# Three cross attentions: how the exponents of the rescaling factors reach all 512 columns

## The chip, the cores and the metric

The kernel runs on one core of one Trainium2 chip. The metric is the time of one execution on the device in microseconds (us); the kernel before was timed three times, and the figure is the median. Lower is better.

## The reference, cut to what matters

The network has four layers, each with a cross attention, a self attention and a feed-forward part; 128 rows of width 256 are updated in place. Three of the four cross attentions (layers 0, 1 and 3) are softmax attentions of the 128 rows over a context of 12544 rows, with 16 heads of width 16. Layer 1 has a key mask; layer 3 turns two columns of the queries before the scores. The reference of layer 1:

```python
qm = _split_heads(q @ Wq.T + bq)
km = _split_heads(k @ Wk.T + bk)
vm = _split_heads(v @ Wv.T + bv)
scores = jnp.einsum('bnlh,bnph->bnlp', qm, km) / np.sqrt(HEAD_DIM).astype(np.float32)
scores = jnp.where(attention_mask[:, None, None, :], scores, MASK_FILL)
attn = jax.nn.softmax(scores, axis=-1)
out = jnp.einsum('bnlp,bnph->bnlh', attn, vm)
```

## The kernel before, in words

One class, `CrossAttention`, computes the three softmax cross attentions, one after the other. The context is cut into 49 chunks of 256 rows. A chunk is projected to keys and values on TensorE (L829, L833). For the softmax a running maximum per query and head is kept: rough scores, made from the rounded queries and keys by 32-row matmuls, four at once in the four row strips of the array (`pe_batch`, L861), are reduced by VectorE (L1288). The exact scores follow six steps later (`pe_unit`, L910, eight units of 512 columns per chunk), ScalarE takes their exponential out of PSUM (L1050), and 17-column matmuls add the weighted values and the sums of the weights to an accumulator that stays in one PSUM bank (`pe_attend`, L946).

The maximum that the scores are shifted by is renewed once in a block of four chunks. One block costs these steps, and the change is in them:

- VectorE, `update_shift`: the maximum over the block (L1297), the shift in two exact halves (L1301, L1302), their sum (L1303), the difference from the last shift (L1307), and that difference in two rounded halves (L1308, L1309). All these are 128x16. The last one sets the semaphore `stage_ready`.
- TensorE, `pe_turned` (L921): the 64 columns of `stage` (two rounded halves of the difference, two exact halves of the shift) are transposed into a PSUM bank.
- ScalarE, `act_turned` (L1085): one copy takes the result to `stage_T` and sets `e_drained`.
- SyncE, `load_shift`: a DMA copies rows 32 to 63 of `stage_T` (the shift) into the packed queries of the next block.
- TensorE, `pe_factor` (L930): four matmuls with 32 rows of `stage_T` as the stationary operand and a 0/1 matrix `spread` as the moving one copy the difference of each head to 32 columns.
- ScalarE, `act_factor` (L1093): its exponential, the factor; VectorE, `rescale` (L1318): the accumulator times the factor.

The order on each engine is written out by hand in `tensor`, `scalar`, `vector` and `gpsimd`. The units (eight of scores, and in every fourth step one "turned" and one "factor") go to two PSUM banks in the order of a list, E_BANK, and a unit waits until the unit before it in its bank is drained by ScalarE (`pe_bank_free`). In a step with a turn, one of the two banks holds in this order score unit 1, turned, score unit 4, factor, score unit 7; the other one score units 0, 2, 3, 5, 6. ScalarE drains in the order turned, units 3, 4, 5, values (L1075), factor, unit 6, unit 7. GpSimd splits each chunk's context (L1204, L1207) and keys (L1222, L1224) into a rounded half and a rest. With 13 blocks there are 13 turns and 12 factors in each cross attention; the last two of each come after the context has been projected. Steps with a turn and a factor while the context is still projected: 10 in each of the three, 30 in all; they are called turn steps below.

In layer 1 (the masked one) VectorE also makes the keys (L1330) and their fill rows; TensorE adds fill terms (L856).

## Time and profile before

| | us |
|---|---|
| median of 3 runs | 1737.86 (1735.96 to 1740.72) |
| the profiled execution, its own time | 1728.72 |
| span of the profiled execution | 1726.9 |
| busy in the span: PE 1569.3 (91%), DVE 1021.3 (59%), ACT 954.8 (55%), POOL 697.5 (40%) | |

PE is TensorE's matmuls, PEld its weight loads, DVE VectorE, ACT ScalarE, POOL GpSimd. A matmul is in flight for longer than it keeps the array from the next one, so the time of a row of matmuls is read from the starts, not from the sum of the durations. In rows a shape such as 32*128 32x256 means 32 rows by 128 columns stationary, 256 columns moving. The three cross attentions concerned lie at about 10 to 440 us, 550 to 985 us and 1255 to 1665 us of the span.

### The profile page before, as it was taken

What the parts mean: (1) busy time and instruction counts of PE and PEld (TensorE: products, weight loads), DVE (VectorE), ACT (ScalarE), POOL (GpSimd) and SP (SyncE); (2) the same over time, 40 slices, a digit from 0 to 9 for tenths busy, and PEclk for the clock granted to TensorE, in tenths of its full rate; (3) what the DMA queues carried; (4) which work ended last, traced back from release to release, by engine and by line L of the source; (5) the groups of instructions that cost most, each with busy time, mean ns of one, the idle gap of its engine ahead of it and who ended that gap; (6) DMA issues with size and microseconds to landing.
All of it is one profiled execution on the core that took longest, in us unless ns stands there. A gap on an engine that the chain in (4) does not pass through costs nothing. (4 is left out here: it accounts for less than half of the span.)

```text
span 1726.9 us, 48550 instructions
## 1 busy us (share of the span) xinstructions
PE 1569.3 (91%) x19973; PEld 1362.8 (79%) x19973; DVE 1021.3 (59%) x1427; ACT 954.8 (55%) x1834; POOL 697.5 (40%) x625
## 2 busy tenths in 40 slices
PE   6999999999777999999999897987499999999965
PEld 5888888888556888888888686876388888888852
DVE  7667787774446877667766252013576666666622
ACT  4677777777313466666666522211167777777742
POOL 5655555551004655555553000000275555555202
PEclk9999999999977999999999998978699999999986
DMA  7665555554045676555554345590365555555430
GB/s 179 176 185 131 127 133 125 127 125 102 1 157 121 182 202 152 143 139 138 142 141 117 96 168 189 202 326 15 95 171 148 135 133 128 131 130 133 102 104 4
DMA packets 149245, 235.42 MB, mean 136 GB/s; under 512 B 24200, under 2 KB 64516, under 8 KB 148100
## 3 DMA queue, kind: packets, MB, share of 16 engines
q1 hardware_dynamic: 141090, 225.09, 49.8%
q10 hardware_dynamic: 7938, 7.23, 1.6%
q8 instruction: 161, 2.64, 0.6%
q14 instruction: 56, 0.46, 0.1%
HBM read 107.06 MB, written 0.23 MB: 62 GB/s over the span
## 5 line engine op out<-in xcount | busy, mean ns | idle before, releaser
L1288 DVE TENSOR_REDUCE L_xattn_maxima<-L_xattn_ps 128x4 f32<-128x1024 f32 x588 | 691.2, 1218 | 337.9 <-PE L_xattn_ps L861 334.1
L1050 ACT ACTIVATE L_xattn_p_ring<-L_xattn_ps 128x512 f32<-128x512 f32 x1176 | 677.6, 598 | 301.5 <-PE L_xattn_ps L910 286.1
L910 PE MATMUL L_xattn_ps<-L_xattn_q_packed,L_xattn_k_packed 128*128 128x256 f32 x2352 | 457.8, 298 | 8.6 <-ACT L_xattn_p_ring L1050 4.7
L910 PEld LDWEIGHTS L_xattn_ps<-L_xattn_q_packed,L_xattn_k_packed 128*128 128x128 f32 x2352 | 337.9, 190 | 65.0 <-issue 29.6
L946 PE MATMUL L_xattn_ps<-L_xattn_p_ring,L_xattn_v_ring 128*17 128x128 f32 x9408 | 289.3, 273 | 1.0 <-ACT L_xattn_p_ring L1050 1.0
L1222 POOL TENSOR_TENSOR L_xattn_k_ring<-L_xattn_k_full,consts 128x512 fp32r<-128x512 f32 x147 | 154.7, 1053 | 279.2 <-ACT L_xattn_k_full L1063 157.8
L829 PE MATMUL L_xattn_ps<-L_xattn_ctx_halves,L_xattn_w_halves 128*128 128x256 f32 x1764 | 261.5, 286 | 0.5 <-POOL L_xattn_ctx_halves L1207 0.4
L946 PEld LDWEIGHTS L_xattn_ps<-L_xattn_p_ring,L_xattn_v_ring 128*17 128x17 f32 x9408 | 242.4, 97 | 23.6 <-ACT L_xattn_p_ring L1050 1.6
L833 PE MATMUL L_xattn_ps<-L_xattn_w_halves,L_xattn_ctx_halves 128*128 128x256 f32 x1764 | 259.9, 285 | 0.0
L829 PEld LDWEIGHTS L_xattn_ps<-L_xattn_ctx_halves,L_xattn_w_halves 128*128 128x128 f32 x1764 | 233.7, 194 | 3.7 <-issue 1.8
L833 PEld LDWEIGHTS L_xattn_ps<-L_xattn_w_halves,L_xattn_ctx_halves 128*128 128x128 f32 x1764 | 232.6, 192 | 2.2 <-issue 0.4
L1204 POOL TENSOR_TENSOR L_xattn_ctx_halves<-L_xattn_ctx_chunk,consts 128x512 fp32r<-128x512 f32 x129 | 134.4, 1042 | 212.6 <-PE L_xattn_ps L833 123.5
L1207 POOL TENSOR_TENSOR L_xattn_ctx_halves<-L_xattn_ctx_chunk,L_xattn_ctx_halves 128x512 fp32r<-128x512 f32 x147 | 190.1, 1293 | 17.9 <-ACT L_xattn_ctx_halves L1128 7.7
L1224 POOL TENSOR_TENSOR L_xattn_k_ring<-L_xattn_k_full,L_xattn_k_ring 128x512 fp32r<-128x512 f32 x147 | 191.0, 1300 | 11.5
L861 PE MATMUL L_xattn_ps<-L_xattn_k_ring,L_xattn_q_hi 32*128 32x256 f32 x2352 | 148.9, 312 | 11.5 <-DVE L_xattn_maxima L1288 7.8
L861 PEld LDWEIGHTS L_xattn_ps<-L_xattn_k_ring,L_xattn_q_hi 32*128 32x128 f32 x2352 | 108.7, 186 | 44.5 <-issue 15.6
L1075 ACT ACTIVATE L_xattn_v_ring<-L_xattn_ps 128x512 f32<-128x512 f32 x147 | 88.0, 599 | 57.2 <-PE L_xattn_ps L833 37.0
L1063 ACT ACTIVATE L_xattn_k_full<-L_xattn_ps,weights 128x256 f32<-128x256 f32 x196 | 81.7, 472 | 12.8 <-PE L_xattn_ps L829 12.8
L233 POOL TENSOR_SCALAR L_attn_rstd<-L_attn_mean_var 128x1 f32<-128x1 f32 x4 | 0.9, 223 | 190.6 <-DVE L_attn_mean_var L222 190.6
L856 PE MATMUL L_xattn_ps<-L_xattn_fill_rows,L_xattn_fill_terms 2*128 2x512 f32 x392 | 52.2, 501 | 3.9 <-DVE L_xattn_maxima L1288 2.1
L1318 DVE TENSOR_TENSOR L_xattn_ps<-L_xattn_ps,L_xattn_factor 128x512 f32<-128x512 f32 x36 | 24.9, 691 | 50.7 <-PE L_xattn_ps L946 50.7
L1330 DVE SCALAR_TENSOR_TENSOR L_xattn_k_full<-L_xattn_ps,weights,L_xattn_mask_chunk 128x256 f32<-128x256 f32 x98 | 42.6, 475 | 1.4 <-PE L_xattn_ps L829 1.0
(365 smaller groups left out, 1109.2 us busy)
## 6 DMA issues: line engine op xcount, KB each, us to landing
L_xattn_k_packed<-L_xattn_k_ring SPq DMA_DIRECT2D x588, 128.0 KB, 2.4
L_xattn_ctx_chunk<-in_ctx_chunks SPq DMA_DIRECT2D x147, 256.0 KB, 3.2
L_xattn_k_packed<-L_xattn_k_ring SPq DMA_DIRECT2D x588, 64.0 KB, 2.1
L_ffn_W<-in_experts_W SPq DMA_DIRECT2D x16, 1024.0 KB, 12.8
L_xattn_mask_chunk<-L_xattn_mask ACTq DMA_DIRECT2D x49, 128.0 KB, 3.1
L_xattn_ctxT<-in_ctxT SPq DMA_DIRECT2D x7, 896.0 KB, 8.5
L_xattn_ctx<-in_ctx SPq DMA_DIRECT2D x7, 896.0 KB, 7.0
weights<-in_pack_L_attn SPq DMA_DIRECT2D x10, 512.0 KB, 4.3
```

What stands on the lines that cost most here:

```text
L829: last = pe.matmul(L.ps[:, KV_BANK, d * KEYS:(d + 1) * KEYS], wk[:, b, e, d * P:(d + 1) * P], x[:, a, e, :], start=start, stop=stop, skip_ ...
L833: last = pe.matmul(L.ps[:, self.v_bank(n), t * D:(t + 1) * D], x[:, a, e, t * P:(t + 1) * P], wv[:, b, e, :], start=start, stop=stop, skip ...
L861: last = pe.matmul(bank[:, r, k * KEYS:(k + 1) * KEYS], self.q_hi[own, 8 * d + 2 * r + k, :], self.k_ring[own, slot, 0, d, :], start=not s ...
L910: last = pe.matmul(L.ps[:, bank, d * 2 * S:(d + 1) * 2 * S], self.k_packed[s][:, quarter, d, half * P:(half + 1) * P], q[:, 2 * pair:2 * p ...
L946: last = pe.matmul(L.ps[q:q + DH + 1, ACC_BANK, col:col + S], self.v_ring[:, m % V_RING, half, h, :], self.p[t % P_RING][:, at, :], start= ...
L1050: act.activation(self.p[t % P_RING][:, 4 * quarter:4 * quarter + 4, :], L.ps[:, E_BANK[unit], :].rearrange("p (h n) -> p h n", n=S), ACT.Exp)\
L1075: act.activation(self.v_ring[:, n % V_RING, :, :, 0:DH].rearrange("p t h n -> p (t h) n"), L.ps[:, self.v_bank(n), :].rearrange("p (m n) - ...
L1204: pool.tensor_tensor(hi, self.ctx_chunk[c][:, :, :], wide(ones[:, 0:DC], KEYS), ALU.mult)\
L1207: pool.tensor_tensor(lo, self.ctx_chunk[c][:, :, :], hi.bitcast(F32), ALU.subtract)\
L1222: pool.tensor_tensor(hi, k[:, :, :], wide(ones[:, 0:DC], KEYS), ALU.mult).then_inc(L["k_hi_ready"], 1)
L1224: pool.tensor_tensor(lo, k[:, :, :], hi.bitcast(F32), ALU.subtract).then_inc(L["k_lo_ready"], 1)
L1288: dve.tensor_reduce(out[:, 4 * v:4 * v + 4], L.ps[:, M_BANK + 2 * v:M_BANK + 2 * v + 2, :] .rearrange("p b (k n) -> p (b k) n", k=2), AX_X ...
```

## The change

The difference of the shifts is now split exactly into three bfloat16 parts on VectorE (five small operations instead of three). It is no longer part of the transposed `stage`, which shrinks to 32 columns with the shift alone. The three parts lie in a 128x128 bfloat16 tile `delta_parts` (five of its eight groups of 16 columns are zero); in all blocks but the first a bfloat16 matmul against the identity transposes it into the same PSUM bank, behind the transpose of `stage`. ScalarE takes the bank out with two copies: `stage_T` (which now sets a semaphore of its own, `stage_turned`, for the DMA) and `delta_T`, 128x128 in bfloat16, which sets `e_drained`. The four matmuls of `pe_factor` read all 128 rows of `delta_T` and a bfloat16 `spread` of 128 rows, whose making at the start of layer 0 takes one more operation on VectorE.

```diff
--- before.py
+++ after.py
@@ -155,7 +155,7 @@
         self.causal_bf = ctx.enter_context(nc.sbuf_tensor("causal_bf", [P, 4, P], BF16))
         self.causal_T_bf = ctx.enter_context(nc.sbuf_tensor("causal_T_bf", [P, 4, P], BF16))
         self.zeros_bf = ctx.enter_context(nc.sbuf_tensor("zeros_bf", [P, BANK], BF16))
-        self.spread = ctx.enter_context(nc.sbuf_tensor("spread", [2 * H, H, 32], F32R))
+        self.spread = ctx.enter_context(nc.sbuf_tensor("spread", [P, H, 32], BF16))
         self.x = ctx.enter_context(nc.sbuf_tensor("x_rows", [S, D], F32))
         self.kv = ctx.enter_context(nc.sbuf_tensor("feature_sums", [64, D + 1], F32))
         self.turn = ctx.enter_context(nc.sbuf_tensor("turn", [P, 24], F32))
@@ -609,10 +609,13 @@
         self.p_ring = sb("p_ring", [P, P_RING, H, S])
         self.p = [self.p_ring[:, c, :, :] for c in range(P_RING)]
         self.maxima = sb("maxima", [S, BLOCK + 2, H])
-        self.shift = sb("shift", [S, 3, H])
-        self.stage = sb("stage", [S, 64])
+        self.shift = sb("shift", [S, 2, H])
+        self.stage = sb("stage", [S, 2 * H])
+        self.delta = sb("delta", [S, 2, H])
+        self.delta_parts = sb("delta_parts", [S, 8, H], BF16)
+        self.delta_T = sb("delta_T", [P, S], BF16)
         self.warm = sb("warm", [P, 2])
-        self.stage_T = sb("stage_T", [64, S], F32R)
+        self.stage_T = sb("stage_T", [2 * H, S], F32R)
         self.factor = sb("factor", [P, 4 * S])
 
         self.q_pairs = self.p_ring[:, 0:2, :, :]
@@ -688,8 +691,11 @@
     def load_shift(self, sp, b):
 
         L = self.L
-        sp.wait_ge(L["e_drained"], E_AT["turned", b] + 1)
-        sp.dma_start(self.q_packed[b % 2][96:98, :, :].bitcast(F32), self.stage_T[32:64, :].bitcast(F32))\
+        if b:
+            sp.wait_ge(L["stage_turned"], b)
+        else:
+            sp.wait_ge(L["e_drained"], E_AT["turned", b] + 1)
+        sp.dma_start(self.q_packed[b % 2][96:98, :, :].bitcast(F32), self.stage_T[:, :].bitcast(F32))\
           .then_inc(L["shift_loaded"], 16)
 
     def fill_tails(self, sp):
@@ -918,8 +924,11 @@
         L, unit = self.L, E_AT["turned", b]
         pe.wait_ge(L["stage_ready"], b + 1)
         self.pe_bank_free(pe, unit)
-        pe.transpose(L.ps[0:64, E_BANK[unit], 0:S], self.stage[:, :], self.net.const("identity"))\
-          .then_inc(L["e_filled"], 1)
+        last = pe.transpose(L.ps[0:2 * H, E_BANK[unit], 0:S], self.stage[:, :], self.net.const("identity"))
+        if b:
+            last = pe.matmul(L.ps[:, E_BANK[unit], S:2 * S], self.delta_parts[:, :, :].rearrange("p a h -> p (a h)"),
+                             self.net.ident_bf[:, :], start=True, stop=True, skip_group_check=True)
+        last.then_inc(L["e_filled"], 1)
 
     def pe_factor(self, pe, b):
 
@@ -929,7 +938,7 @@
         for i in range(4):
             last = pe.matmul(L.ps[:, E_BANK[unit], i * S:(i + 1) * S],
                              self.net.spread[:, 4 * i:4 * i + 4, :].rearrange("p h n -> p (h n)"),
-                             self.stage_T[0:2 * H, :], start=True, stop=True, skip_group_check=True)
+                             self.delta_T[:, :], start=True, stop=True, skip_group_check=True)
         last.then_inc(L["e_filled"], 1)
 
     def pe_attend(self, pe, m, half):
@@ -1082,7 +1091,11 @@
         act.wait_ge(L["e_filled"], unit + 1)
         if b:
             act.wait_ge(L["shift_loaded"], 16 * b)
-        act.activation(self.stage_T[:, :], L.ps[0:64, E_BANK[unit], 0:S], ACT.Copy).then_inc(L["e_drained"], 1)
+        last = act.activation(self.stage_T[:, :], L.ps[0:2 * H, E_BANK[unit], 0:S], ACT.Copy)
+        if b:
+            last.then_inc(L["stage_turned"], 1)
+            last = act.activation(self.delta_T[:, :], L.ps[:, E_BANK[unit], S:2 * S], ACT.Copy)
+        last.then_inc(L["e_drained"], 1)
 
     def act_factor(self, act, b):
 
@@ -1103,7 +1116,10 @@
         if self.first:
             identity = net.const("identity")
             dve.tensor_copy(net.ident_bf[:, :], identity).then_inc(L["constants_made"], 1)
-            dve.tensor_tensor(net.spread[:, :, :], wide(identity[0:2 * H, 0:H], 32), wide(identity[0:2 * H, H:2 * H], 32),
+            dve.tensor_tensor(self.delta_T[:, 0:H], identity[:, 0:H], identity[:, H:2 * H], ALU.add)\
+               .then_inc(L["parts_placed"], 1)
+            dve.wait_ge(L["parts_placed"], 1)
+            dve.tensor_tensor(net.spread[:, :, :], wide(self.delta_T[:, 0:H], 32), wide(identity[:, 2 * H:3 * H], 32),
                               ALU.add).then_inc(L["constants_made"], 1)
             dve.tensor_copy(net.causal_bf[:, :, :], times(net.const("causal"), 4)).then_inc(L["constants_made"], 1)
             dve.tensor_copy(net.causal_T_bf[:, :, :], times(net.const("causal_T"), 4)).then_inc(L["constants_made"], 1)
@@ -1292,21 +1308,23 @@
 
         L, stage, first = self.L, self.stage, b % 2
         most = self.maxima[:, (BLOCK + 1) * (1 - first), :]
-        one, two = stage[:, 32:48].bitcast(F32R), stage[:, 48:64].bitcast(F32R)
+        one, two = stage[:, 0:H].bitcast(F32R), stage[:, H:2 * H].bitcast(F32R)
         dve.wait_ge(L["batch_reduced"], 4 * min(BLOCK * (b + 1), NCHUNK))
         o.after(dve.tensor_reduce(most, self.maxima[:, first:first + BLOCK + 1, :].rearrange("p s h -> p h s"), AX_X,
                                   ALU.max))
         if b:
             dve.wait_ge(L["e_filled"], E_AT["turned", b - 1] + 1)
         o.after(dve.tensor_scalar(one, most, -1.0, None, ALU.mult))
-        o.after(dve.scalar_tensor_tensor(two, most, -1.0, stage[:, 32:48], ALU.mult, ALU.subtract))
-        last = dve.tensor_tensor(self.shift[:, b % 2, :], stage[:, 32:48], stage[:, 48:64], ALU.add)
+        o.after(dve.scalar_tensor_tensor(two, most, -1.0, stage[:, 0:H], ALU.mult, ALU.subtract))
+        last = dve.tensor_tensor(self.shift[:, b % 2, :], stage[:, 0:H], stage[:, H:2 * H], ALU.add)
         if b:
             o.after(last)
-            delta = self.shift[:, 2, :]
+            delta, rest, parts = self.delta[:, 0, :], self.delta[:, 1, :], self.delta_parts
             o.after(dve.tensor_tensor(delta, self.shift[:, b % 2, :], self.shift[:, 1 - b % 2, :], ALU.subtract))
-            o.after(dve.tensor_copy(stage[:, 0:H].bitcast(F32R), delta))
-            last = dve.tensor_tensor(stage[:, H:2 * H], delta, stage[:, 0:H], ALU.subtract)
+            o.after(dve.tensor_copy(parts[:, 0, :], delta))
+            o.after(dve.tensor_tensor(rest, delta, parts[:, 0, :], ALU.subtract))
+            o.after(dve.tensor_copy(parts[:, 1, :], rest))
+            last = dve.tensor_tensor(parts[:, 2, :], rest, parts[:, 1, :], ALU.subtract)
         last.then_inc(L["stage_ready"], 1)
         dve.wait_ge(L["stage_ready"], b + 1)
 
@@ -1354,7 +1372,7 @@
         if not self.dequantizing:
             self.norm.vector_rows(dve)
         self.net.wait_weights(dve, L.name)
-        dve.memset(self.stage[:, 0:32], 0.0)
+        dve.memset(self.delta_parts[:, :, :], 0.0)
         o.after(dve.memset(self.maxima[:, :, :], -LARGEST))
         dve.wait_ge(L["q_in_psum"], 1)
         if self.turned:
```

TensorE around one turn and factor, layer 0, step of the second turn, before (`stage` is transposed by L921, the factor's exponents are made by L930):

```order
L946 MATMUL L_xattn_ps<-L_xattn_p_ring,L_xattn_v_ring 17x128 x32
L921 MATMUL L_xattn_ps<-consts,L_xattn_stage 64x128
L910 MATMUL L_xattn_ps<-L_xattn_q_packed,L_xattn_k_packed 128x256 x4
L833 MATMUL L_xattn_ps<-L_xattn_w_halves,L_xattn_ctx_halves 128x256 x6
L910 MATMUL L_xattn_ps<-L_xattn_q_packed,L_xattn_k_packed 128x256 x2
L833 MATMUL L_xattn_ps<-L_xattn_w_halves,L_xattn_ctx_halves 128x256 x6
L930 MATMUL L_xattn_ps<-L_xattn_stage_T,spread 128x128 x4
L910 MATMUL L_xattn_ps<-L_xattn_q_packed,L_xattn_k_packed 128x256 x2
```

and the same place now:

```order
L955 MATMUL L_xattn_ps<-L_xattn_p_ring,L_xattn_v_ring 17x128 x32
L927 MATMUL L_xattn_ps<-consts,L_xattn_stage 32x128
L929 MATMUL L_xattn_ps<-ident_bf,L_xattn_delta_parts 128x128
L916 MATMUL L_xattn_ps<-L_xattn_q_packed,L_xattn_k_packed 128x256 x4
L839 MATMUL L_xattn_ps<-L_xattn_w_halves,L_xattn_ctx_halves 128x256 x6
L916 MATMUL L_xattn_ps<-L_xattn_q_packed,L_xattn_k_packed 128x256 x2
L839 MATMUL L_xattn_ps<-L_xattn_w_halves,L_xattn_ctx_halves 128x256 x6
L939 MATMUL L_xattn_ps<-L_xattn_delta_T,spread 128x128 x4
L916 MATMUL L_xattn_ps<-L_xattn_q_packed,L_xattn_k_packed 128x256 x2
```

One matmul has come in behind the transpose; nothing else has changed its place.

VectorE in the step before, where the shift is renewed, before:

```order
L1297 TENSOR_REDUCE L_xattn_maxima<-L_xattn_maxima 128x16
L1301 TENSOR_SCALAR L_xattn_stage<-L_xattn_maxima 128x16
L1302 SCALAR_TENSOR_TENSOR L_xattn_stage<-L_xattn_maxima,L_xattn_stage 128x16
L1303 TENSOR_TENSOR L_xattn_shift<-L_xattn_stage 128x16
L1307 TENSOR_TENSOR L_xattn_shift<-L_xattn_shift 128x16
L1308 CAST L_xattn_stage<-L_xattn_shift 128x16
L1309 TENSOR_TENSOR L_xattn_stage<-L_xattn_shift,L_xattn_stage 128x16
```

and now:

```order
L1313 TENSOR_REDUCE L_xattn_maxima<-L_xattn_maxima 128x16
L1317 TENSOR_SCALAR L_xattn_stage<-L_xattn_maxima 128x16
L1318 SCALAR_TENSOR_TENSOR L_xattn_stage<-L_xattn_maxima,L_xattn_stage 128x16
L1319 TENSOR_TENSOR L_xattn_shift<-L_xattn_stage 128x16
L1323 TENSOR_TENSOR L_xattn_delta<-L_xattn_shift 128x16
L1324 CAST L_xattn_delta_parts<-L_xattn_delta 128x16
L1325 TENSOR_TENSOR L_xattn_delta<-L_xattn_delta,L_xattn_delta_parts 128x16
L1326 CAST L_xattn_delta_parts<-L_xattn_delta 128x16
L1327 TENSOR_TENSOR L_xattn_delta_parts<-L_xattn_delta,L_xattn_delta_parts 128x16
```

The chain that ends with `stage_ready` is two operations longer, and each waits for the one before it.

ScalarE in the turn step, before:

```order
L1085 ACTIVATE L_xattn_stage_T<-L_xattn_ps 64x128
L1050 ACTIVATE L_xattn_p_ring<-L_xattn_ps 128x512 x3
L1075 ACTIVATE L_xattn_v_ring<-L_xattn_ps 128x32x16
L1093 ACTIVATE L_xattn_factor<-L_xattn_ps 128x512
L1050 ACTIVATE L_xattn_p_ring<-L_xattn_ps 128x512 x4
```

and now:

```order
L1094 ACTIVATE L_xattn_stage_T<-L_xattn_ps 32x128
L1097 ACTIVATE L_xattn_delta_T<-L_xattn_ps 128x128
L1059 ACTIVATE L_xattn_p_ring<-L_xattn_ps 128x512 x3
L1084 ACTIVATE L_xattn_v_ring<-L_xattn_ps 128x32x16
L1106 ACTIVATE L_xattn_factor<-L_xattn_ps 128x512
```

The second copy stands in front of the exponential of unit 3.

## Rows read from the trace of the kernel before

**Rows 1.** Busy time over 60:405, 605:950 and 1300:1630, the sum of the three.
```profile
sum 1020.00, PE 1015.04 PEld 907.39 DVE 710.13 ACT 704.17 POOL 545.95; mean PE 338.35 PEld 302.46 DVE 236.71 ACT 234.72 POOL 181.98
```

**Rows 2.** By line L1085 and L1309: durations (min/median/max), and waiters (us, times).
```profile
  PEld L_xattn_ps L910: 9.5, 30
...
L1309 DVE TENSOR_TENSOR L_xattn_stage<-L_xattn_shift,L_xattn_stage x36: 174/176/1062, 74.6 to 1640.6; 128x16 f32<-128x16 f32 x36
...
  PEld L_xattn_ps L921: 2.3, 10
```

**Rows 3.** TensorE in order of time, turn step of layer 0 (start, us, group).
```profile
108.56 0.30 PE L921 MATMUL L_xattn_ps<-consts,L_xattn_stage 128*64 128x128 f32 x1
...
109.56 0.87 PE L833 MATMUL L_xattn_ps<-L_xattn_w_halves,L_xattn_ctx_halves 128*128 128x256 f32 x6
...
111.32 0.66 PE L930 MATMUL L_xattn_ps<-L_xattn_stage_T,spread 32*128 32x128 f32 x4
...
112.78 0.51 PE L910 MATMUL L_xattn_ps<-L_xattn_q_packed,L_xattn_k_packed 128*128 128x256 f32 x2
113.12 0.64 PE L829 MATMUL L_xattn_ps<-L_xattn_ctx_halves,L_xattn_w_halves 128*128 128x256 f32 x4
```

**Rows 4.** TensorE, the step after it, without a turn.
```profile
117.69 0.74 PE L910 MATMUL L_xattn_ps<-L_xattn_q_packed,L_xattn_k_packed 128*128 128x256 f32 x4
118.28 0.88 PE L833 MATMUL L_xattn_ps<-L_xattn_w_halves,L_xattn_ctx_halves 128*128 128x256 f32 x6
...
121.06 0.64 PE L829 MATMUL L_xattn_ps<-L_xattn_ctx_halves,L_xattn_w_halves 128*128 128x256 f32 x4
```

**Rows 5.** ScalarE in the turn step of rows 3.
```profile
108.89 0.27 ACT L1085 ACTIVATE L_xattn_stage_T<-L_xattn_ps 64x128 fp32r<-64x128 f32 x1 [0.98 <-PE L_xattn_ps L921]
109.13 1.29 ACT L1050 ACTIVATE L_xattn_p_ring<-L_xattn_ps 128x512 f32<-128x512 f32 x2
...
112.01 0.60 ACT L1093 ACTIVATE L_xattn_factor<-L_xattn_ps 128x512 f32<-128x512 f32 x1
```

**Rows 6.** ScalarE and TensorE in a turn step of layer 1.
```profile
711.69 0.60 ACT L1093 ACTIVATE L_xattn_factor<-L_xattn_ps 128x512 f32<-128x512 f32 x1
...
712.69 0.50 PE L910 MATMUL L_xattn_ps<-L_xattn_q_packed,L_xattn_k_packed 128*128 128x256 f32 x2
```

**Rows 7.** VectorE and GpSimd before the turn of rows 3.
```profile
107.50 0.18 DVE L1309 TENSOR_TENSOR L_xattn_stage<-L_xattn_shift,L_xattn_stage 128x16 f32<-128x16 f32 x1
...
107.51 1.08 POOL L1222 TENSOR_TENSOR L_xattn_k_ring<-L_xattn_k_full,consts 128x512 fp32r<-128x512 f32 x1 [1.87 <-ACT L_xattn_k_full L1063]
```

**Rows 8.** VectorE and GpSimd before the turn at 241.5, layer 0.
```profile
240.45 0.99 DVE L1309 TENSOR_TENSOR L_xattn_stage<-L_xattn_shift,L_xattn_stage 128x16 f32<-128x16 f32 x1
...
240.38 1.04 POOL L1222 TENSOR_TENSOR L_xattn_k_ring<-L_xattn_k_full,consts 128x512 fp32r<-128x512 f32 x1 [1.90 <-DMA L_xattn_k_packed<-L_xattn_k_ring]
241.49 1.28 POOL L1224 TENSOR_TENSOR L_xattn_k_ring<-L_xattn_k_full,L_xattn_k_ring 128x512 fp32r<-128x512 f32 x1
```

**Rows 9.** VectorE and GpSimd before the turn at 208.3, layer 0.
```profile
207.05 0.90 DVE L1308 CAST L_xattn_stage<-L_xattn_shift 128x16 fp32r<-128x16 f32 x1
207.98 0.17 DVE L1309 TENSOR_TENSOR L_xattn_stage<-L_xattn_shift,L_xattn_stage 128x16 f32<-128x16 f32 x1
208.19 2.35 DVE L1288 TENSOR_REDUCE L_xattn_maxima<-L_xattn_ps 128x4 f32<-128x1024 f32 x2
...
206.84 1.08 POOL L1222 TENSOR_TENSOR L_xattn_k_ring<-L_xattn_k_full,consts 128x512 fp32r<-128x512 f32 x1 [1.62 <-ACT L_xattn_k_full L1063]
208.00 1.30 POOL L1224 TENSOR_TENSOR L_xattn_k_ring<-L_xattn_k_full,L_xattn_k_ring 128x512 fp32r<-128x512 f32 x1
```

**Rows 10.** GpSimd in layer 1, in the turn step of rows 6.
```profile
708.10 1.04 POOL L1222 TENSOR_TENSOR L_xattn_k_ring<-L_xattn_k_full,consts 128x512 fp32r<-128x512 f32 x1 [3.31 <-DVE L_xattn_k_full L1330]
```

**Rows 11.** By line L869: the bfloat16 matmuls with 128 columns near the end of layer 0's cross attention.
```profile
L869 PE MATMUL L_xattn_ps<-causal_bf,ident_bf x16: 219/219/230, 406.1 to 412.0; 128*128 128x128 bf16 x16
```

**Rows 12.** TensorE near the start of layer 0.
```profile
22.18 0.79 PE L861 MATMUL L_xattn_ps<-L_xattn_k_ring,L_xattn_q_hi 32*128 32x256 f32 x4 [2.88 <-DVE L_xattn_maxima L1288]
```

## The prediction

> **What bounds the kernel.** I read the busy times of the three stages first, then TensorE in order of time through one step with a turn and one without, then ScalarE and VectorE beside GpSimd in the same stretch, and the waits of the lines that change.
>
> Over 1020 us of the three softmax cross attentions a matmul is in flight for 1015.0, VectorE is busy for 710, ScalarE for 704, GpSimd for 546 [rows 1]. So in these stages TensorE sets the pace, and what counts is only what makes it start later. The reader should look at starts. In the turn step of layer 0 the stretch from the transpose (108.56) to the next projection (113.12) takes 4.56 us; the same stretch without a turn takes 3.37, from 117.69 to 121.06 [rows 3, 4]. A turn and its factor cost TensorE 1.19 us. Of this 0.41 is the turn: 1.00 us from 108.56 to 109.56 against 0.59 from 117.69 to 118.28 [rows 3, 4]. The factor costs the other 0.78.
>
> TensorE waits in one place of each turn: score unit 4 takes the PSUM bank that the turned block held, and cannot start before ScalarE has copied it out. 30 weight loads waited 9.5 us for that copy, 0.32 each [rows 2]. In 10 turns TensorE waited for VectorE's last operation before the turn as well (2.3 us in all) [rows 2]. Their durations show why: the median is 176 ns, the longest 1062, for 128x16 values. Where it is long, GpSimd was running.
>
> **The factor's matmuls (a gain).** The four 32-row matmuls go from 111.32 on; from the projection before them to the rough scores after them there are a change from 128 rows to 32 and one back. By the starts the whole costs 0.78. In bfloat16 with 128 rows both changes go. What is left are four matmuls of 128 columns; at 128 columns against 256 they need at most what the others do. Bounds for the saving on TensorE: 0.78 at most, nothing at least; I take 0.50 (an estimate: 0.28 stays for four short matmuls, at 0.06 to 0.07 each, half the 0.12 of a 256-column matmul: a group of six takes 0.88, one of four 0.64 [rows 4]).
>
> But this saving runs into ScalarE. Score unit 7 takes the factor's PSUM bank, so it cannot start before the exponential of the factor ends. That starts at 112.01, right behind the drain of the values on ScalarE, which is tied to the projection before the factor and does not come earlier; it ends at 112.61 [rows 5]. With 0.05 for the release (an estimate) unit 7 can start at 112.66. It starts at 112.78 now [rows 3]. Of the 0.50 only 0.12 arrives: 20 turn steps in layers 0 and 3, -2.4 us. In layer 1 the fill matmuls lie between: the exponential ends at 712.29, unit 7 starts at 712.69 [rows 6], and 0.35 arrives: 10 x 0.35 = -3.5 us.
>
> **The second copy (a loss in all 30 turns).** `e_drained` now comes with the second of two copies. One copy takes 0.27, and the next operation on ScalarE starts 0.24 behind it (108.89, 109.13) [rows 5]. TensorE already waits for this copy, with nothing to cover it, so all 0.24 counts. The added matmul delays the first copy: at least by nothing (its own time in flight is 219 ns for such a bfloat16 matmul [rows 11], against 0.30 for the transpose [rows 3]), at most by 0.15, for a change from the narrow transpose to 128 columns. I take 0.06: together +0.30, bounds 0.24 and 0.39. 30 x 0.30 = 9.0 us. The exponentials of units 3 and 4 come later by the same, which TensorE's own delay covers. The DMA of the shift hangs on the first copy and is not later against TensorE.
>
> Here the Trainium skill has a rule that would make it dearer (TensorEngine Tiling (Array Packing), Key Properties): a change of tiling mode drains TensorE. The transpose narrows from 64 columns to 32, the width class of the 17-column matmuls before it, so by the rule one drain would only move behind the transpose; in the trace a turn costs 0.41, of which 0.32 is the wait for the copy, so the narrow transpose and all changes around it cost only 0.09 [rows 2 to 4]. By the rule the upper bound of 0.39 would hold, 2.7 us more in all; no run here shows this pair yet.
>
> **The longer chain on VectorE (a loss in up to 20 turns).** Two more operations of 128x16, at a pitch of 0.21 (207.98 to 208.19) [rows 9]: 0.42. Where nothing disturbs them, this is hidden: before the turn at 108.56 the chain ended at 107.68 [rows 7], 0.88 early [rows 3]. In layer 1 the keys are made behind the chain, and GpSimd starts only after them [rows 10]; there the cover holds and the cost is nothing. In layers 0 and 3 GpSimd starts its split of the keys just as the chain ends. The two do not share: at 240.45 the last operation took 0.99 instead of 0.18, and it ended at 241.44, 0.02 behind GpSimd's 1.04 from 240.38 [rows 8]; a cast started at 207.05 behind GpSimd's start at 206.84 took 0.90 [rows 9]. The next VectorE operation then went in front of GpSimd's second one (207.98 against 208.00), and after that GpSimd runs for 1.28 to 1.30 [rows 8, 9].
>
> So there are two cases, by who is first.
> - *VectorE first* (rows 7: 107.50 against 107.51; 10 turns, those of layers 0 and 3 that did not wait). Now the third of the five operations stands there. The fourth, a cast, waits for the end of GpSimd's 1.08 at 108.59 and ends at 108.62; the fifth slips in before the second GpSimd operation, as at 207.98, and ends at 108.83. With 0.06 to TensorE the turn starts at 108.89 instead of 108.56: +0.33, with the second copy +0.63. The 0.33 is 3.3 us over 10 turns.
> - *GpSimd first* (the 10 turns that waited). The third operation ends at 241.44, the fourth goes in front of GpSimd's second one (241.49), the fifth is held until that ends: 241.49 + 1.28 + 0.03 = 242.80, where the chain ended at 241.44 before. +1.36 on a wait that already has no cover: 10 x 1.36 = 13.6 us.
>
> The Trainium skill has this as a rule (SBUF — State Buffer, SBUF: two separate sides): VectorE operations with two SBUF inputs or in a two-port mode and GpSimd operations exclude each other for whole instructions, whoever comes first. It also counts a cast among the operations that take the pair; the rows show this for a cast to fp32r only. Were a cast to bfloat16 free, the first case would cost 0.21 less each, 2.1 us in all; the second one would not change, since its fifth operation has two inputs.
>
> **The rest.** At the start of layer 0 one more VectorE operation stands before the first reductions, for which TensorE waited 2.88 us at 22.18 [rows 12]. At least 0.1; at most one more held operation, 1.3 as above. I take 0.8. The six turns and factors behind the last projection: TensorE gains 0.2 to 0.5 on a factor, and waits for the longer copy; nothing, between -1 and +1. The width of `stage` and the zeroing cost nothing that shows.
>
> **Sum.** 9.0 + 3.3 + 13.6 - 2.4 - 3.5 + 0.8 = +20.8 us. The profiled execution took 1728.7, so it would take 1749.5; the median of the runs is 9.1 above that execution, and the same difference on 1737.9 gives 1758.7. I predict 1759.
>
> **Rivals.**
> - *VectorE first in all 20 turns of layers 0 and 3.* The order is decided by 0.01 us (107.50 and 107.51), so it can tip. 9.0 + 20 x 0.33 - 5.9 + 0.8 = +10.5: 1748. Against: before the change 10 of 20 lost, in the same phase. 15 in 100.
> - *GpSimd first in nearly all 20.* 9.0 + 20 x 1.36 - 5.1 = +31: 1769. Same argument the other way. 12 in 100.
> - *The added operations are not held* (a small bfloat16 cast or difference passes beside GpSimd). Then the chain is longer by 0.42 only, hidden in the first case: 9.0 + 10 x 0.42 - 5.9 + 0.8 = +8: 1746. Against: the row of the cast. 8 in 100.
> - *No change:* the chain is covered everywhere and the second copy costs 0.24: 7.2 - 5.9 = +1.3, 1739. It needs a VectorE that starts the chain earlier; in 10 turns it is already late. 8 in 100.
> - *Faster:* unit 7 does not wait for the factor's exponential, because the drain of the values comes earlier than I think, and the whole 0.50 arrives in 30 steps: -15.0, with 9.0 for the copies -6: 1732. It decides as soon as unit 7 starts less than 0.05 behind the factor's exponential. Against: the exponential starts where the drain ends, not where the last factor matmul ends. It also needs the chain on VectorE to be hidden. 6 in 100.
>
> The forecast itself has 51 in 100; its own range, with the bounds of the copies (-1.8, +2.7), the cast (-2.1), the start (-0.7, +0.5), the tails (1) and two turns tipping either way (2), is 1754 to 1764. The range for 8 in 10 takes in the first two rivals: 1745 to 1771. A measurement of this kernel can tell 0.3% (5.2 us) from no change. Faster by more: 0.07. Within: 0.11. Slower: 0.82.
>
> **What would show it.** Right: the wait of unit 4's weight load for the second copy near 0.6 us in each of the 30 turns; `delta_T` starting 0.24 behind `stage_T`; the last operation of the chain (L1327) with a longest duration near 1.1 to 1.3 us and ten or so TensorE waits for it of about 1.4 us; unit 7 right behind the factor's exponential. Blocks of four steps in layer 1 as long as before. Wrong: the four factor matmuls followed by a unit 7 that does not wait; no long duration in the chain although GpSimd runs; a turn pitch in layers 0 and 3 that is the one of before.

## The result, and the profile after

| | before | changed |
|---|---|---|
| median of 20 runs, us | 1737.84 (1732.89 to 1742.88) | 1750.22 (1738.54 to 1758.89) |
| ratio, 95% interval | | 1.0071 (1.0057 to 1.0085) |
| profiled execution, span, us | 1726.9 | 1748.9 |

The change makes the kernel 12.4 us slower by the medians. The two profiled executions differ by 22.0 us, and the difference between these two numbers is part of what had to be found out.

Where the time went shows in the first and last start of the score matmuls of each of the three cross attentions. These are the groups of their line by line, in the windows 0:500, 500:1100 and 1200:1720, for the kernel before (the two numbers ahead of the semicolon are the first and the last start):

```profile
L910 PE MATMUL L_xattn_ps<-L_xattn_q_packed,L_xattn_k_packed x784: 274/283/468, 48.6 to 435.0; 128*128 128x256 f32 x196
L910 PE MATMUL L_xattn_ps<-L_xattn_q_packed,L_xattn_k_packed x784: 274/283/388, 576.0 to 978.2; 128*128 128x256 f32 x196
L910 PE MATMUL L_xattn_ps<-L_xattn_q_packed,L_xattn_k_packed x784: 274/283/388, 1275.6 to 1658.0; 128*128 128x256 f32 x196
```

and for the changed one:

```profile
L916 PE MATMUL L_xattn_ps<-L_xattn_q_packed,L_xattn_k_packed x784: 274/283/467, 48.0 to 445.9; 128*128 128x256 f32 x196
L916 PE MATMUL L_xattn_ps<-L_xattn_q_packed,L_xattn_k_packed x784: 274/283/390, 594.3 to 993.5; 128*128 128x256 f32 x196
L916 PE MATMUL L_xattn_ps<-L_xattn_q_packed,L_xattn_k_packed x784: 274/283/388, 1291.6 to 1678.7; 128*128 128x256 f32 x196
```

The three stages took 386.4, 402.2 and 382.4 us before (1171.0) and take 397.9, 399.2 and 387.1 now (1184.2): +11.5, -3.0, +4.7, together +13.2 (from starts given to 0.1 us; unrounded it is 13.0). The masked one, layer 1, is faster. That is the change's own effect in these two executions. Of the rest of the 22.0 us, 7.5 lie between the first and the second stage (435.0 to 576.0 before, 445.9 to 594.3 now), where of the change there is only the zeroing of its new tile (0.11 us where it was 0.09) and the first turn of layer 1.

The medians differ by about as much, 12.4, but not for this reason alone. Of the 20 executions of the changed kernel three had a mean granted clock of 0.945 or more of full speed, of a later 20 of the kernel before (timed beside e1) eight. Among the executions at 0.942 or less the medians are 1750.6 (17 of them) and 1740.8 (12): about 10 us. At one and the same clock, 0.937, the changed kernel took from 1750.0 to 1758.9, where the kernel before at 0.937 or 0.938 took 1741.7 to 1742.6. That fits a number of held turns that differs between executions, of which the profile is one draw; only one execution of the changed kernel was profiled, so this is not shown.

The places that the prediction spoke of, in the changed kernel. VectorE, GpSimd and TensorE at a turn of layer 0 where GpSimd came first, from the timeline (start, duration, group, idle time before it and its releaser) [rows 8]:

```profile
244.99 1.00 DVE L1325 TENSOR_TENSOR L_xattn_delta<-L_xattn_delta,L_xattn_delta_parts 128x16 f32<-128x16 f32 x1
246.03 0.17 DVE L1326 CAST L_xattn_delta_parts<-L_xattn_delta 128x16 bf16<-128x16 f32 x1
246.24 1.12 DVE L1327 TENSOR_TENSOR L_xattn_delta_parts<-L_xattn_delta,L_xattn_delta_parts 128x16 bf16<-128x16 f32 x1
...
244.92 1.04 POOL L1238 TENSOR_TENSOR L_xattn_k_ring<-L_xattn_k_full,consts 128x512 fp32r<-128x512 f32 x1 [1.90 <-DMA L_xattn_k_packed<-L_xattn_k_ring]
246.04 1.28 POOL L1240 TENSOR_TENSOR L_xattn_k_ring<-L_xattn_k_full,L_xattn_k_ring 128x512 fp32r<-128x512 f32 x1
...
247.41 0.28 PE L927 MATMUL L_xattn_ps<-consts,L_xattn_stage 128*32 128x128 f32 x1 [1.29 <-DVE L_xattn_delta_parts L1327]
247.53 0.22 PE L929 MATMUL L_xattn_ps<-ident_bf,L_xattn_delta_parts 128*128 128x128 bf16 x1
```

The third operation of the chain is held until GpSimd's first one ends, the fourth slips in 0.01 us ahead of GpSimd's second one, the fifth is held until that ends at 247.32, and TensorE idles for 1.29 us. At a turn of layer 3 where VectorE came first [rows 7]:

```profile
1352.17 0.90 DVE L1326 CAST L_xattn_delta_parts<-L_xattn_delta 128x16 bf16<-128x16 f32 x1
1353.11 0.17 DVE L1327 TENSOR_TENSOR L_xattn_delta_parts<-L_xattn_delta,L_xattn_delta_parts 128x16 bf16<-128x16 f32 x1
...
1351.96 1.08 POOL L1238 TENSOR_TENSOR L_xattn_k_ring<-L_xattn_k_full,consts 128x512 fp32r<-128x512 f32 x1 [1.91 <-ACT L_xattn_k_full L1072]
1353.12 1.29 POOL L1240 TENSOR_TENSOR L_xattn_k_ring<-L_xattn_k_full,L_xattn_k_ring 128x512 fp32r<-128x512 f32 x1
...
1353.34 0.28 PE L927 MATMUL L_xattn_ps<-consts,L_xattn_stage 128*32 128x128 f32 x1 [0.25 <-DVE L_xattn_delta_parts L1327]
```

Only the cast is held, and the last operation goes 0.01 us ahead of GpSimd's. Over the whole kernel the line of the last operation says [rows 2]:

```profile
L1327 DVE TENSOR_TENSOR L_xattn_delta_parts<-L_xattn_delta,L_xattn_delta_parts x36: 174/176/1118, 75.4 to 1661.9; 128x16 bf16<-128x16 f32 x36
...
  PEld L_xattn_ps L927: 22.3, 20
```

All 20 turns of layers 0 and 3 wait for it now, 22.3 us in all against 2.3 in 10 turns [rows 2]. In 11 of the 20 the last operation was held (nine in layer 0, two in layer 3); the longest took 1118 ns.

A turn step of layer 1, TensorE and ScalarE [rows 6]; nothing holds VectorE there:

```profile
725.83 0.28 PE L927 MATMUL L_xattn_ps<-consts,L_xattn_stage 128*32 128x128 f32 x1
725.95 0.22 PE L929 MATMUL L_xattn_ps<-ident_bf,L_xattn_delta_parts 128*128 128x128 bf16 x1
...
726.68 0.50 PE L916 MATMUL L_xattn_ps<-L_xattn_q_packed,L_xattn_k_packed 128*128 128x256 f32 x2 [0.23 <-ACT L_xattn_delta_T L1097]
727.02 0.88 PE L839 MATMUL L_xattn_ps<-L_xattn_w_halves,L_xattn_ctx_halves 128*128 128x256 f32 x6
...
728.70 0.40 PE L939 MATMUL L_xattn_ps<-L_xattn_delta_T,spread 128*128 128x128 bf16 x4
728.91 0.48 PE L916 MATMUL L_xattn_ps<-L_xattn_q_packed,L_xattn_k_packed 128*128 128x256 f32 x2
...
730.03 0.50 PE L916 MATMUL L_xattn_ps<-L_xattn_q_packed,L_xattn_k_packed 128*128 128x256 f32 x2
730.37 0.64 PE L835 MATMUL L_xattn_ps<-L_xattn_ctx_halves,L_xattn_w_halves 128*128 128x256 f32 x4
...
726.21 0.27 ACT L1094 ACTIVATE L_xattn_stage_T<-L_xattn_ps 32x128 fp32r<-32x128 f32 x1 [2.00 <-PE L_xattn_ps L929]
726.38 0.25 ACT L1097 ACTIVATE L_xattn_delta_T<-L_xattn_ps 128x128 bf16<-128x128 f32 x1
...
728.89 0.60 ACT L1084 ACTIVATE L_xattn_v_ring<-L_xattn_ps 128x512 f32<-128x512 f32 x1
729.39 0.59 ACT L1106 ACTIVATE L_xattn_factor<-L_xattn_ps 128x512 f32<-128x512 f32 x1
```

From the transpose to the next projection it is 1.19 us (725.83 to 727.02) against 1.00 before [rows 3]: the second copy and the added matmul together cost 0.19. The four factor matmuls are through in 0.21 (728.70 to 728.91) against 0.58 (111.32 to 111.90 by the timeline of before). Unit 7 starts at 730.03, 0.05 behind the end of the factor's exponential (729.98).

The drain of the values before the factor's exponential of rows 5, before the change, and the projection groups before and behind a factor of layer 0, changed:

```profile
111.42 0.60 ACT L1075 ACTIVATE L_xattn_v_ring<-L_xattn_ps 128x512 f32<-128x512 f32 x1
```

```profile
249.57 0.88 PE L839 MATMUL L_xattn_ps<-L_xattn_w_halves,L_xattn_ctx_halves 128*128 128x256 f32 x6
...
251.96 0.64 PE L835 MATMUL L_xattn_ps<-L_xattn_ctx_halves,L_xattn_w_halves 128*128 128x256 f32 x4
```

And the wait near the start of layer 0, changed [rows 12]:

```profile
21.68 0.50 PE L867 MATMUL L_xattn_ps<-L_xattn_k_ring,L_xattn_q_hi 32*128 32x256 f32 x4 [3.09 <-DVE L_xattn_maxima L1304]
```

### The profile page after: what moved, and what is told of

It reads as the page before. It is cut to its first block and busy times, and to the rows that moved or that the text cites. A ratio compares the mean times of both kernels' runs of the same rounds, so it can differ in the third digit from the quotient of the medians.

```text
span 1748.9 us, 48723 instructions
## 1 busy us (share of the span) xinstructions
PE 1568.1 (90%) x20001; PEld 1364.4 (78%) x20009; DVE 1053.1 (60%) x1500; ACT 954.3 (55%) x1870; POOL 698.3 (40%) x625
## 5 line engine op out<-in xcount | busy, mean ns | idle before, releaser
L1240 POOL TENSOR_TENSOR L_xattn_k_ring<-L_xattn_k_full,L_xattn_k_ring 128x512 fp32r<-128x512 f32 x147 | 191.2, 1301 | 11.5
L1094 ACT ACTIVATE L_xattn_stage_T<-L_xattn_ps 32x128 fp32r<-32x128 f32 x39 | 10.3, 265 | 62.2 <-PE L_xattn_ps L929 58.9
## 6 DMA issues: line engine op xcount, KB each, us to landing
L_ffn_W<-in_experts_W SPq DMA_DIRECT2D x16, 1024.0 KB, 12.8
```

What stands on the lines that cost most here:

```text
L1240: pool.tensor_tensor(lo, k[:, :, :], hi.bitcast(F32), ALU.subtract).then_inc(L["k_lo_ready"], 1)
```

## The experiments

Stage lengths below are read as above, from first to last score matmul; "the three stages" is their sum. The cost of a turn is TensorE's time from the last value-weighting matmul of the step to the next projection, less the same stretch of a step without a turn: 0.42 us before (0.49 in three of the 30 turns); after the change 0.61 in layer 1, and in layers 0 and 3 0.92 to 0.94 (nine turns) or 1.97 to 2.04 (eleven).

**e1: the factor's matmuls alone, whole-array but in fp32r.** Rows 32 to 127 of the 0/1 matrix and rows 64 to 127 of `stage_T` are zero. ScalarE's copy and VectorE's making of the matrix keep to the rows that they filled before; these lines are left out here, as `...` says.

```diff
-        self.spread = ... "spread", [2 * H, H, 32], F32R
+        self.spread = ... "spread", [P, H, 32], F32R
...
-        self.stage_T = sb("stage_T", [64, S], F32R)
+        self.stage_T = sb("stage_T", [P, S], F32R)
...
-                             self.stage_T[0:2 * H, :], start=True, ...
+                             self.stage_T[:, :], start=True, ...
...
+        if self.first:
+            for r in range(32, P, 32):
+                dve.memset(net.spread[r:r + 32, :, :].bitcast(F32), 0.0)
+        dve.memset(self.stage_T[64:P, :].bitcast(F32), 0.0)
```

> The kernel before with one edit: the factor's four matmuls use all 128 rows in fp32r (rows 32 to 127 of the 0/1 matrix and 64 to 127 of stage_T are zero); transpose, single copy and VectorE's chain as before. Theory (the gain is the change of row mode, limited by ScalarE's exponential): score unit 7 starts 0.21 us earlier in 20 turn steps and 0.45 in 10, together -8.7 us, a median near 1729. Rival 1 (the gain comes from bfloat16, fp32r matmuls of 128 columns at 0.11 each hold TensorE): -3 us or less. Rival 2 (the factor is off the path, all of it is hidden): 0.

Measured: median 1722.3 us, ratio to before 0.9928 (0.9899 to 0.9956). The three stages take 1162.7 us, 8.4 less than before. A turn costs 0.42 as before (0.47 to 0.49 in four). ScalarE and TensorE around a factor of layer 0:

```profile
110.44 0.56 PE L930 MATMUL L_xattn_ps<-L_xattn_stage_T,spread 128*128 128x128 f32 x4
...
111.78 0.50 PE L910 MATMUL L_xattn_ps<-L_xattn_q_packed,L_xattn_k_packed 128*128 128x256 f32 x2
...
110.64 0.60 ACT L1075 ACTIVATE L_xattn_v_ring<-L_xattn_ps 128x512 f32<-128x512 f32 x1
111.13 0.59 ACT L1093 ACTIVATE L_xattn_factor<-L_xattn_ps 128x512 f32<-128x512 f32 x1
```

From the factor's first matmul to unit 7 it is 1.34 us, against 1.46 before [rows 3]. With the 0.09 by which the factor starts sooner behind the projection this gives the 0.21 expected. In layer 1 the gain is 0.34 per factor (3.4 in the stage) and not 0.45, since four matmuls in fp32r take 0.39 (110.44 to 110.83) where bfloat16 takes 0.21. So the gain is the one of the rows, bfloat16 adds 0.11 in layer 1 and nothing in the other two, where the exponential limits both. Rivals 1 and 2 are out. Nor are the 32-row matmuls slow in themselves: by the single starts they follow each other by 0.11 us, as the 128-row ones do. What goes is at the two changes of rows: the factor's first matmul started 0.21 behind the projection and starts 0.12 behind it, the second followed by 0.17 and follows by 0.06, the first matmul behind the factor followed by 0.20 and follows by 0.11, the one after it by 0.22 and now 0.17. Together this is the 0.34.

The median fell by 16.3, more than the stages, because four of the six executions had a granted clock of 0.946 or 0.947, and only eight of the 20 of the kernel before 0.945 to 0.947. These alone compared, the medians are 1721.7 and 1733.2: 11.4 us. Where the 3 us between this and the 8.4 of the profiles lie was not looked into.

**e2: the changed kernel, GpSimd kept out of the chain's way.**

```diff
         def split_keys(n):
+            if block_turned(n):
+                pool.wait_ge(L["stage_ready"], block_turned(n) + 1)
```

> The changed kernel with one more wait: in turn steps GpSimd's split of the keys starts only after stage_ready, so it cannot hold VectorE's chain. Theory (11 turns lose 1.4 us and 9 lose 0.3 to GpSimd): all turns of layers 0 and 3 cost TensorE about 0.2 us as in layer 1, -18 us against the changed kernel, a median near 1732; the last operation of the chain never over 0.2 us. Rival (the longer chain itself is what costs, or GpSimd's delay is paid later by keys that come late): the turns still wait for VectorE, or the stages get longer elsewhere; not under 1745.

Measured: median 1733.3 us, ratio to before 0.9973 (0.9955 to 0.999), 16.9 under the changed kernel. The last operation of the chain:

```profile
L1329 DVE TENSOR_TENSOR L_xattn_delta_parts<-L_xattn_delta,L_xattn_delta_parts x36: 174/175/176, 75.1 to 1647.7; 128x16 bf16<-128x16 f32 x36
```

Never over 176 ns, and no TensorE wait for it is left. All 30 turns cost 0.61 or 0.62. The three stages take 1167.4 us, 16.8 less than in the changed kernel and 3.6 less than in the kernel before, and nothing came back elsewhere in them. GpSimd holding VectorE is the whole cost of the longer chain; the two added operations as such cost nothing.

**e3: the kernel before, with the chain two operations longer.** (The tile `extra` is declared beside `stage`.)

```diff
+            o.after(dve.tensor_tensor(self.extra[:, 0, :], delta, stage[:, 0:H], ALU.subtract))
+            o.after(dve.tensor_copy(self.extra[:, 1, :].bitcast(F32R), self.extra[:, 0, :]))
             last = dve.tensor_tensor(stage[:, H:2 * H], delta, stage[:, 0:H], ALU.subtract)
```

> The kernel before with two more 128x16 operations (a difference and a cast, unused) in VectorE's chain, nothing else. Theory (GpSimd takes the turn between them): the last operation is held for 1.1 us or more in about half of the 20 turns of layers 0 and 3, where the turn comes 1.4 us later, and comes 0.3 later in the others; +17 us (10 to 27). Rival (no hold, only 0.42 us more of chain): +4 us, and no turn later by over 0.5.

Measured: median 1761.7 us, ratio 1.0131 (1.0104 to 1.0159). The three stages take 1192.6 us, +21.5.

```profile
L1312 DVE TENSOR_TENSOR L_xattn_stage<-L_xattn_shift,L_xattn_stage x36: 174/176/1117, 77.6 to 1672.7; 128x16 f32<-128x16 f32 x36
...
  PEld L_xattn_ps L922: 22.6, 20
```

Nearly the same as in the changed kernel, with no bfloat16 in the chain: again 20 turns wait. Ten of them have the last operation held, and in one more (the first of layer 0) it is the fourth, the added cast, that is held for 1.12 and the last one follows at once. These eleven cost 1.76 to 2.13, the other nine 0.73 to 0.75. The count of held turns was forecast as half; the stages grew by 4 us more than 17, which lies in the range given.

**e4: the kernel before, with a second copy.** (The tile `extra_T`, 128x128 in bfloat16, is declared beside `stage`.)

```diff
-        act.activation(self.stage_T[:, :], ...).then_inc(L["e_drained"], 1)
+        last = act.activation(self.stage_T[:, :], ...)
+        if b:
+            last = act.activation(self.extra_T[:, :], L.ps[:, E_BANK[unit], 0:S], ACT.Copy)
+        last.then_inc(L["e_drained"], 1)
```

> The kernel before with a second, unused ScalarE copy (128x128 to bfloat16) before the PSUM bank is given free. Theory (the wait of score unit 4 has no cover): each of 30 turns costs 0.17 to 0.24 us more, +5 to +7 us. Rival (the copy overlaps the first one or the unit is late anyway): 0.

Measured: median 1745.7 us, ratio 1.0046 (1.0027 to 1.0065). The three stages +7.1 us. An undisturbed turn costs 0.58 instead of 0.42: 0.16 for the copy, a little under the range given for it. 30 times that is 4.8; one turn of layer 0 cost 1.58, with VectorE's chain held by chance, as in a repeat of the kernel before (e7), and that makes up for another 1.0. The other 1.3 were not taken apart. The copy is not hidden.

**e5: e1 and the wait of e2 together, in the kernel before.**

> The fp32r whole-array version of e1 with the wait of e2 (GpSimd's split of the keys starts after stage_ready in turn steps). Theory: in e1 only three or four turns were 0.05 to 0.07 us late by GpSimd, so the wait has 0.2 us to give and costs nothing: the three stages within 1 us of e1's 1162.7. Rival (GpSimd's later start is paid somewhere): the stages 2 us longer or more.

Measured: median 1727.2 us, ratio 0.9931 (0.9906 to 0.9957). The three stages take 1161.9 us, 0.8 less than in e1, and every turn costs 0.42. As expected; in time e1 and e5 cannot be told apart.

**e6: the changed kernel with two parts instead of three.**

```diff
-            o.after(dve.tensor_tensor(rest, delta, parts[:, 0, :], ALU.subtract))
-            o.after(dve.tensor_copy(parts[:, 1, :], rest))
-            last = dve.tensor_tensor(parts[:, 2, :], rest, parts[:, 1, :], ALU.subtract)
+            last = dve.tensor_tensor(parts[:, 1, :], delta, parts[:, 0, :], ALU.subtract)
```

> The changed kernel without the third bfloat16 part (the low bits of the difference are left out): VectorE's chain has three operations behind the shift, as before the change. Theory: no operation is left to be held; turns cost TensorE 0.61 us in all stages as in layer 1 (0.07 more where GpSimd is first), stages near 1168, a median near 1733. Rival (what costs is bfloat16 output beside GpSimd, not the number of operations): turns of 0.9 or 2.0 remain in layers 0 and 3.

Measured: median 1732.4 us, ratio 0.9966 (0.9949 to 0.9983). The three stages 1166.9 us; all turns 0.61 to 0.68. The bfloat16 output is not the cause; the place of the fourth and fifth operation is. (This kernel leaves out the low bits of the difference.)

**e7: the kernel before, profiled again.**

> The kernel before, unchanged, for a second profile. The first one took 1728.7 us, 4 us under the fastest of 20 timed runs. Theory (the stretch between the first and the second of these cross attentions varies from run to run with TensorE's clock): the three stages are 1171 us again, within 1, and that stretch is 148 us instead of 141, with more time at the lower clock. Rival (the stages themselves vary): they differ by over 3 us.

Measured: 1738.7 us. The three stages take 1172.7 us (387.7, 402.3, 382.7) against 1171.0: 1.7 more, where within 1 was expected, and 1.0 of it is one turn of layer 0 with VectorE held. The stretch between the first and second stage follows, by windows. The columns are the window and its length, busy time and number of instructions of PE, PEld, DVE, ACT and POOL, then the granted clock as a share of full speed, the DMA share and GB/s; first the profile of before, then e7:

```profile
435.00:575.90 140.90, 103.58 (x693) 82.35 (x692) 78.98 (x135) 32.39 (x65) 32.10 (x35) 0.84 0.36 103
```

```profile
435.70:582.40 146.70, 111.64 (x693) 90.33 (x692) 79.06 (x135) 32.42 (x65) 32.02 (x35) 0.78 0.35 99
```

The same 693 matmuls: 146.7 us at a granted clock of 0.78 where it was 140.9 at 0.84. In the changed kernel it is 148.4 at 0.76 (690 matmuls recorded of the same ones):

```profile
445.90:594.30 148.40, 112.63 (x690) 91.72 (x692) 79.20 (x135) 32.31 (x65) 32.14 (x35) 0.76 0.34 98
```

The other profiles fall into the same two groups: 140.6 at 0.84 in e1, and in e3, e4 and e5, all three made from the kernel before, 148.0, 148.6 and 148.2 at 0.75 to 0.77. So the first profile of before was one in which this stretch was at the full clock for longer, and the extra 7.5 us between the two profiles are not the change's.

## Why the prediction was right or wrong

The direction, the range and the mechanism held: 1750 lies in 1745 to 1771, the kernel is slower, and each place that the prediction named shows in the trace. The number alone would not show that: the first rival, VectorE first in all 20 turns, came to 1748. It is the eleven held turns that rule it out. The most likely value, +20.8 us, was too high against +13.2 in the stages and +12.4 in the medians.

e2 parts the sum in two. Without the holds the stages are 3.6 us shorter than before, where the terms for copy and factor gave +3.1 (9.0 - 2.4 - 3.5); this is nearly all of the miss (with the sizes measured below it is 5.7 - 8.9 - 0.6 = -3.8). The holds add 16.8, where the chain's two terms gave 16.9. Mis-sized were three terms: the factor's gain, the second copy, and the start. By the prediction's own steps:

- *The factor's matmuls.* The 0.50 on TensorE was right: in layer 0 0.22 of it arrives, and unit 7 then waits for another 0.27 (at the 0.44 behind the first rough scores that it took before it would start at 251.35, and it starts at 251.62). That unit 7 waits for the exponential was right too. Mis-sized: what arrives. Forecast 0.12 and 0.35, measured 0.22 (projection 110.51 to 113.12 before, 249.57 to 251.96 now) and 0.45 (710.19 to 713.03, and 727.98 to 730.37). The step that failed is "right behind the drain of the values": 111.42 + 0.60 met 112.01 by coincidence. On ScalarE the next operation starts 0.50 behind such a drain (728.89 to 729.39; 110.64 to 111.13 in e1), not 0.60; before, the exponential came 0.03 behind the end of the last factor matmul (111.32 + 0.66 = 111.98 [rows 3]), for which it was waiting. 20 x 0.22 + 10 x 0.45 = -8.9, where -5.9 was forecast.
- *The second copy.* In the path, as said, in all 30 turns (e4). Forecast 0.30, measured 0.19, under the lower bound of 0.24. The second copy starts 0.17 behind the first (726.21 to 726.38), where I took the 0.24 between a copy and an exponential, and it is 0.02 shorter than the one copy of before (0.25, 0.27). The delay of the first copy was about right: it starts 0.38 behind the transpose (725.83 to 726.21) where it was 0.33 [rows 3, 5], so 0.05, forecast 0.06. The wait of unit 4's weight load for the second copy, forecast near 0.6, is 12.8 us in 30 turns, 0.43 each. The rule of the Trainium skill on changes of tiling mode (TensorEngine Tiling (Array Packing), Key Properties) gave the high end, 0.39, by a 0.15 for which no row stood; the bfloat16 matmul starts 0.12 behind the narrow transpose (725.83, 725.95), so the measured turn speaks against it for this pair. 30 x 0.19 = 5.7, where 9.0 was forecast.
- *The longer chain.* Both cases are in the trace operation for operation. VectorE first: forecast +0.33, measured 0.31 to 0.32 (0.92 to 0.94 less 0.61). GpSimd first: forecast +1.36, measured 1.36 to 1.43 (1.97 to 2.04 less 0.61). The ten turns forecast for this case were eleven. The rule of the Trainium skill on the exclusive pair (SBUF — State Buffer, SBUF: two separate sides) holds, and for the cast to bfloat16 too: it was held for 0.90 at 1352.17. e2 and e6 take it away from two sides and e3 puts it into the kernel before. That rival 3 (not held) is wrong is shown.
- *Which turns tip.* That the order can tip was said, which turns do was not foreseen: in layer 0 the two turns that VectorE had won went to GpSimd and one went the other way; in layer 3 GpSimd won two of ten again, but other ones. The order hangs on 0.01 us and changes from kernel to kernel and, in e7, between executions of the same kernel.
- *The start of layer 0.* Forecast +0.8. TensorE's wait of rows 12 is 3.09 us where it was 2.88, and 2.88 again in e7: +0.21; from the first projection of the layer to the end of this wait it is 10.71 us (10.97 to 21.68) where it was 10.66 (11.52 to 22.18), so +0.05. Both are near the bound of 0.1, and 0.8 was too much. The added operation is in fact long, 1.27 us (17.73 to 19.00), but making `spread` behind it takes 0.69 (19.04) where it took 1.79 (18.44), which the term left out. That the first score matmul starts at 48.0 instead of 48.6 says nothing, since in e7 the kernel before starts it at 48.1.
- *The steps behind the last projection.* Forecast nothing, between -1 and +1. In e2, and as much in the changed kernel, each stage takes 0.2 less from its twelfth turn to its last score matmul (27.07 before, 26.87 after in layer 0): -0.6 in all. A block of four steps in layer 1, forecast as long as before, is 0.28 shorter (34.83, 34.55), by the same sizes of factor and copy.
- *From the profile to the median.* The 9.1 us between before's profiled execution and its median were added as if every execution of the changed kernel had them. They were mostly a matter of TensorE's clock in that one execution: e7, the same kernel, took 10.0 us more, 7.6 of it between the stages. For the median it was harmless, since the sum was against before's median. But that the prediction's 1749.5 for the profiled execution stands next to the 1750.7 that it took is luck: 22 us between two profiles, of which 13 are the change's.

With the measured sizes the terms are 5.7 + 9 x 0.32 + 11 x 1.40 - 8.9 = +15.1 us for the 30 turn steps; the stages show 13.2. Of the 1.9 that are missing 0.6 lie behind the last projection. The chain's two terms, 18.3 here, are 16.8 in the stages by e2, so about 1.5 of the holds is made up elsewhere in the steps; where, was not taken apart.

## What to carry to other kernels

The two changes of rows around four 32-row matmuls cost TensorE 0.34 us here (e1), and padding these matmuls with zeros to 128 rows is a cheap way out: e1 does it with no other edit and is 0.7% faster than before (0.4 to 1.0%), where the change under study paid for the same gain with a longer chain and a second copy. Before adding small VectorE operations to a chain that TensorE waits for, look at what GpSimd runs at that time: an operation of 0.17 us can take 1.1. Moving GpSimd's work behind the chain gave that back (e2). And two profiles are compared stage by stage, since a stretch that the change hardly touches can differ by 7 us.

## What the runs showed of the hardware that was not expected

- ScalarE overlaps operations out of PSUM: behind a 128x512 operation of 0.60 us the next one starts after 0.50 (728.89, 729.39), behind a copy of 128 columns of 0.27 after 0.17 (726.21, 726.38).
- After a held operation VectorE gets exactly one in before GpSimd's next one starts, 0.01 to 0.02 us ahead (246.03 against 246.04, 1353.11 against 1353.12; 207.98 against 208.00 before [rows 9]). In a chain of dependent small operations beside two GpSimd operations in a row every second one is held, here the third and the fifth (244.99, 246.24).
- A matmul of 32 rows and 128 columns keeps the array from the next one for 0.11 us in fp32r, as one of 128 rows does; the time that e1 saves lies at the changes from one to the other.
